# Contraction rows of one kind of attention product in a hybrid layer: 32 cut to 16 and 17

## The reference, cut to what matters

```python
def _mha(q, k, v, wq, wk, wv, wo):           # a node of the cell, H = 8, dh = 16
    qh = (q @ wq).reshape(B, S, H, dh)
    kh = (k @ wk).reshape(B, S, H, dh)
    vh = (v @ wv).reshape(B, S, H, dh)
    scores = jnp.einsum('bqhd,bkhd->bhqk', qh, kh) / jnp.sqrt(jnp.asarray(dh, q.dtype))
    attn = jax.nn.softmax(scores, axis=-1)
    ctx = jnp.einsum('bhqk,bkhd->bqhd', attn, vh).reshape(B, S, d)
    return ctx @ wo

# the cell
for c in range(NUM_NOD):                     # 6 nodes
    ...
    q = ew[c, 0] * (nodes[in_q] @ We[eq] + be[eq])
    k = ew[c, 1] * (nodes[in_k] @ We[ek] + be[ek])
    v = ew[c, 2] * (nodes[in_v] @ We[ev] + be[ev])
    nodes[c] = act_w[c] * _mha(q, k, v, Wq[c], Wk[c], Wv[c], Wo[c]) + q
```

## Time and profile before

| | |
|---|---|
| median of 3 runs | 1783.27 us (1781.34 to 1786.0) |
| profiled execution, its own time | 1786.0 us |
| its span, first to last instruction | 1784.2 us |
| TensorE matmuls busy | 1325.5 us, 74% |
| VectorE busy | 1068.9 us, 60% |
| ScalarE busy | 743.8 us, 42% |
| granted TensorE clock, mean | 0.846 |

### The profile page before, as it was taken

How to read it: one execution, slowest core, us unless ns; L and a number is a source line. 1 busy time by engine, 2 the same in 40 slices (tenths; PEclk the granted TensorE clock), 3 DMA queues, 4 the chain that set the end, 5 groups by cost and what they waited for, 6 DMA issues and landing times.

```text
span 1784.2 us, 28722 instructions
## 1 busy us (share of the span) xinstructions
PE 1325.5 (74%) x10896; PEld 909.0 (51%) x10896; DVE 1068.9 (60%) x1757; ACT 743.8 (42%) x1420; POOL 272.1 (15%) x276
## 2 busy tenths in 40 slices
PE   6647766778597759877697759876896859778527
PEld 5424444445485437644584437544673538446417
DVE  2312324496368737785568736784669636876674
ACT  0123333455355535544445535543455534544323
POOL 0000001022101201031102201031102201121160
PEclk9677887779798879979898879879898979879858
DMA  4051021001210031002210032002210131001201
GB/s 158 22 57 20 2 30 17 1 13 23 45 63 5 22 54 55 16 13 27 55 52 1 25 51 67 4 14 31 62 40 6 27 49 60 4 14 54 74 1 63
DMA packets 199511, 62.20 MB, mean 35 GB/s; under 512 B 169232, under 2 KB 181296, under 8 KB 199248
## 3 DMA queue, kind: packets, MB, share of 16 engines
q1 hardware_dynamic: 199376, 60.36, 15.5%
HBM read 54.02 MB, written 5.80 MB: 34 GB/s over the span
## 4 chain that ended last, share of the span: by engine, by line
PE 49%; DVE 17%; SPq 14%; issue 8%; ACT 8%; DMA 3%; POOL 1%; DVEq 0%; ACTq 0%; POOLq 0%
SPq L585 12%; PE strips L802 9%; PE ps L963 6%; PE ps L975 6%; PE strips L784 5%; PE attn_out L815 5%; DVE hb L1448 4%; ACT probs L1066 4%; DVE rowmax_B L1307 3%; DVE hb L1443 2%; PE ps L644 2%; DVE rowmax_A L1307 2%; PE ps L740 2%; DVE work L1417 2%; SPq L605 1%
## 5 line engine op out<-in xcount | busy, mean ns | idle before, releaser
L1066 ACT ACTIVATE probs<-strips 128x1024 f32<-128x1024 f32 x256 | 248.9, 1021 | 278.6 <-PE strips L802 277.0
L1307 DVE TENSOR_REDUCE rowmax_B<-strips 128x4 f32<-128x1024 f32 x192 | 227.2, 1219 | 131.8 <-PE strips L784 131.7
L802 PE MATMUL strips<-qs_b,ks_b 32*128 32x256 f32 x1536 | 139.3, 486 | 210.5 <-DMA qs_b<-maxrow_B 140.3
L802 PEld LDWEIGHTS strips<-qs_b,ks_b 32*128 32x128 f32 x1536 | 87.9, 226 | 242.8 <-DMA qs_b<-maxrow_B 142.9
L1448 DVE TENSOR_TENSOR_SCAN hb<-da,hb 128x1024 f32<-128x1024 f32 x64 | 151.6, 2368 | 2.2
L1534 DVE SCALAR_TENSOR_TENSOR work<-hb,ps 128x512 f32<-128x512 f32 x128 | 86.6, 686 | 96.6 <-ACT hb L1192 96.1
L784 PE MATMUL strips<-ks_b,qs_b 32*128 32x256 f32 x1536 | 126.7, 449 | 23.2 <-ACT probs L1066 12.4
L975 PE MATMUL ps<-ze,w_e 128*128 128x256 f32 x512 | 127.4, 386 | 3.0 <-DVE work L1534 1.8
L963 PE MATMUL ps<-w_e,work 128*128 128x128 f32 x1024 | 125.1, 277 | 1.2 <-DVE work L1534 1.2
L963 PEld LDWEIGHTS ps<-w_e,work 128*128 128x128 f32 x1024 | 121.2, 192 | 8.1 <-DVE work L1534 4.4
L815 PE MATMUL attn_out<-probs,vb 128*32 128x256 f32 x1536 | 115.5, 430 | 5.2 <-ACT probs L1066 5.0
(11 more groups left out here) (259 smaller groups left out, 2213.5 us busy)
## 6 DMA issues: line engine op xcount, KB each, us to landing
w_e<-in_w_e SPq DMA_DIRECT2D x128, 256.0 KB, 3.1
qs_a<-a_scr SPq DMA_DIRECT2D x32, 128.0 KB
ks_a<-a_scr SPq DMA_DIRECT2D x32, 128.0 KB
a_scr<-qkv_a SPq DMA_DIRECT2D x8, 384.0 KB, 2.5
pos<-t_scr SPq DMA_DIRECT2D x8, 264.0 KB, 11.0
qs_b<-maxrow_B SPq DMA_DIRECT2D x96, 4.0 KB
probs<-in_b_we_t SPq DMA_DIRECT2D x1, 1280.0 KB, 7.0
x_in<-in_x SPq DMA_DIRECT2D x8, 128.0 KB, 2.7
```

The lines of the kernel that those rows point to most:

```text
L802: mm = pe.matmul(o, strip(ks, b, kind, g, j, rows, kc * P, P), strip(qs, b, kind, g, j, rows, 0, L), start=True, stop=True)
L1066: act.activation(probs[:, group % 2, 2 * i:2 * i + 2, :, :].rearrange("p h a b -> p (h a b)"), strips[i][:, :], ACT.Exp).then_inc(s_exp, 1)
L1307: dve.tensor_reduce(out=rowmax[kind][:, b % sides_n, k % 2, 2 * i:2 * i + 2, :], in_=strips[i][:, :].rearrange("p (h q t) -> p h q t", h=2 ...
```

## The change

In `maximum` the products of kind B contract over 16 partitions of each strip, and in `score` over 17. Kind A keeps its 8 and 9. No instruction is added, removed or moved on any engine; each of the B products at L784 and L802, matmul and weight load alike, reads fewer partitions. The results are the same, since the partitions left out hold zeros.

```diff
@@ maximum
-                rows = STRIP if kind == "B" else AW
+                rows = BW if kind == "B" else AW
                 take_strips(b, "max", kind, g)
@@ score
-                rows = STRIP if kind == "B" else AW + 1
+                rows = (BW if kind == "B" else AW) + 1
                 take_strips(b, "score", kind, g)
```

## The result

The changed kernel takes 1832.84 us (median of 4 runs, 1828.89 to 1842.26) against 1783.23 us before: a ratio of 1.0285, 95% interval 1.0239 to 1.0332, or about 50 us more. The forecast was slower by 20 us, with 1832 as the end of the range; the median lies just beyond it. The direction was right, the amount 2.5 times too small. The before times of later runs go from 1773.79 to 1794.69 us, so a few microseconds mean nothing here. One trace of an experiment (burst16) was taken in a disturbed execution; only stretches of it are read.

What follows compares the result with a forecast made beforehand. Bound by laps of dense TensorE work, waits for VectorE's scan or ScalarE, and one long SP wait. Bursts and other engines 0; 20 places x 3.4 us = 68 us low, at 0.30 = 20 us; 1783.3 + 20 = 1804, range 1784 to 1832.

Steps and rivals of the forecast that it cites:

- A burst keeps its length: Bursts at L784 and L802 stay at 1.15 us (high clock) and 2.09 us (low) with fewer rows: 0 us.
- Fewer rows hold the clock less: On TensorE, a burst using few rows does less to raise or hold the granted clock, though equally busy.
- pairs of stretches: Trace stretches with A or B bursts, TensorE about equally busy (3.18 against 3.19 us), yet opposite clock outcomes.
- The price of a low microsecond: Time lost per microsecond at the low clock: 0.30 us, from two laps giving 0.26 and an upper bound of 0.45.
- At each place I let the clock be low for 3.4 us more: Each of 20 places, 12 clock rises and 8 holding stretches, gets the trace's shortest low spell: 68 us low.
- The steady laps: Four laps after 600 us, with about one place a lap where the clock is lost for 3.4 us more.
- ten places of 3.4 us: The early part before 415 us, where places are dense: ten of the 20, each 3.4 us more low.
- The rival of laps that lock differently: Spells shift into later stages of each lap: 40 places of 3.4 us at 0.33, 45 us, 1828; chance 0.15.
- The rivals without effect and faster: Clock ignores rows or waits hide it: 1783, 0 to 4 us more, chance 0.19; shorter bursts: 1764, chance 0.05.
- The signs: If right: mean clock 0.82 to 0.83, unchanged burst lengths and instruction counts, laps 1 to 3 us longer, mostly early.
- The rise behind the long wait: After TensorE's wait for a transfer queued behind SP's gathers (L585), the clock rises one or two bursts later.

Runs made afterwards that it cites:

- burst16: Kernel before, with 18 repeats of the kind B burst, 16 rows a strip, in TensorE's wait of about 18 us: 1790.90 us, ratio 1.0018.
- burst8: Kernel before, with 18 repeats of the burst, 8 rows a strip, in TensorE's wait of about 18 us: 1836.96 us, ratio 1.0296.
- burst32: Kernel before, with 18 repeats of the burst, 32 rows a strip, in TensorE's wait of about 18 us: 1774.97 us, ratio 0.9959.
- a32: Kernel before, with kind A given 32 rows in place of 8 and 9 in both bursts, the added rows zeros: 1769.06 us, ratio 0.9932.
- score17: Kernel before, with only kind B's second burst (L802) cut to 17 rows, the first keeping 32: 1813.20 us, ratio 1.0186.
- keep4: Changed kernel, with 32 rows given back to 4 of 12 groups of kind B in the second burst (L802): 1805.58 us, ratio 1.0134.
- rows24: Kernel before, with 24 rows in place of 32 in both bursts of kind B: 1812.72 us, ratio 1.0187.
- max16: Kernel before, with only kind B's first burst (L784) cut to 16 rows, the second keeping 32: 1791.89 us, ratio 1.0061.
- warm: Kernel before, with 36 full products in front of the L802 burst that waits about 18 us, seven sequences: 1771.30 us, ratio 0.9942.

## Why the prediction was wrong, point by point

- **A burst keeps its length: right.** 1.15 and 2.09 us with 16, 17 and 24 rows.
- **Fewer rows hold the clock less: right, and now shown.** In the forecast it was read from pairs of stretches that differed in other things too. burst8 and burst32 differ in the rows alone, the stretch behind the long wait differs before and after in the rows of its bursts, and a32 shows the gain of more rows.
- **The price of a low microsecond: near enough, if anything too high.** 0.30 was taken; 42.9 / 152 = 0.28 was measured. From one trace each, score17 gives (1813.6 - 1784.2) / (653 - 550) = 0.29, keep4 20.4 / 71 = 0.29, rows24 24.3 / 72 = 0.34, but max16 9.1 / 17 = 0.5 and a32 14.9 / 79 = 0.19. With the medians of the spans and low times of all executions it is 0.23 to 0.25 for max16, score17, keep4 and rows24, and 0.19 for a32. It is no price for every place: in warm the low time falls by 109 us and the span by 6, since most of it was low while TensorE only waited.
- **"At each place I let the clock be low for 3.4 us more": this step failed.** 20 places of 3.4 us made 68 us; the trace has 152. The term that was mis-sized is how long a spell lasts once it has begun. I took the shortest spell of the trace, as if the clock came back at once. burst16 shows why it need not: bursts of 16 rows held a high clock, but without a pause for 30.8 us they didn't raise a low one. The stretch from 1015.1 stayed low for 20.3 us until other work came, and behind the long wait 11 us passed; one lap earlier the same bursts held the high clock. That the short bursts are what kept it low there is read from this likeness and from keep4; the value products between them, with 128 rows and 32 columns, were not tested alone.
- **The steady laps: failed for the same reason.** I gave them one short spell each, 4 x 3.4 = 14 us low and some 4 us of time. Between the L926 of the second and of the sixth sequence the low time grew by 75 us and the time by 22.7 us (789.4 to 812.1). That is 19 of the 23 us by which the forecast fell short in the span. Three of these laps got the 20 us spell and take 205 us. The rest came out near the forecast: up to the first L926 11.6 us more (426.4 to 438.0) and 44 us more low, where ten places of 3.4 us gave 34 us and 10 us of time. The stretch was before me: it is the one that I showed as holding. I asked whether it would fall and put a short fall on it; I didn't ask what would raise the clock there again.
- **The rival of laps that lock differently** priced nearly the measured amount (1828). A lap did lengthen because spells came at the same point in each. But not from more places of 3.4 us: from long spells at few places, 46 spells in all in place of 47. That it came so near in number is luck.
- **The rivals without effect and faster: wrong**, by the ratio and by the burst lengths.
- **The signs.** The rise behind the long wait came two bursts later, as said. The mean clock is 0.808, below the 0.82 to 0.83 given, and the laps that changed most are longer by 7 to 9 us, not by 1 to 3.

What stays open is why the spell at 1015 comes from the third steady lap on and not in the two before, which have the same work in the same order; score17, with the same rows in these bursts, has it in one lap only. What decides between them was not tried. Nor was it tried whether the rows in a strip count or the rows of all four strips together.

## What to carry to other kernels

When a burst gets cheaper for TensorE without getting shorter, look at the granted clock: here the zeros in unused rows were worth 50 us, and 24 and 23 more rows of zeros for the other kind another 12. Price a lost clock not by the number of falls but by what follows each: count the time until work comes that can raise it again. Where TensorE idles in front of a chain of short bursts, throwaway work that ended before the wait did cost nothing that showed here, and it kept the clock for what follows; in burst8 it outlasted the wait and cost 53 us.

## What the runs showed of the hardware that was not expected

- With TensorE busy without a pause, the granted clock depended on the rows of the matmuls: 4 strips of 32 rows raised it and held it, 4 strips of 8 rows did neither, 4 strips of 16 rows held 1.00 for 15.7 us (six of six) but stayed at 0.50 for 30.8 us when they began there (one of one).
- Rows that hold zeros count too: cutting B's 15 or 16 zero rows lowered the mean clock from 0.846 to 0.808, and adding zero rows to A raised it to 0.867 in a32.
- Discarded work can pay: 36 products in a wait, about 15.8 us of TensorE's time in each of seven sequences, made the kernel 10 us faster.
